# Windowed attention scores on four 32x32 parts of TensorE in place of two 64x64 parts, with the q tiles written by ScalarE and not placed by DMA

## The reference, cut to what matters

```python
q = Wq @ layernorm(x) + bq;  k = Wk @ ctx + bk;  v = Wv @ ctx + bv      # 128 x 1024
k, v padded by 8 left and 7 right                                       # WINDOW = 16
dots[h, t, w] = sum_d q[h, d, t] * k[h, d, t + w] / sqrt(16)            # 8 heads of 16 channels
out[h, d, t]  = sum_w softmax_w(dots)[h, t, w] * v[h, d, t + w]
x = x + Wo @ out + bo
z = layernorm(x);  gate = softmax(z @ gate_w.T), the best 2 of 8, renormed
x = x + sum_e w[:, e] * (z @ A[e].T @ B[e].T)                           # rank 64, 8 experts
```

## Time and profile before

| | before |
|---|---|
| device time, median of 3 runs | 1184.99 us (1182.85 to 1186.56) |
| device time of the profiled execution | 1181.87 us |
| its span, first to last instruction | 1180.1 us |
| TensorE matmuls busy, weight loads busy | 1118.5 us (95%), 965.0 us (82%) |
| VectorE, ScalarE, GpSimd busy | 904.6, 391.8, 408.9 us |
| matmul records on line 342 (scores) | 8192, busy 264.0 us |
| DMAs of `place_q` | 256 of 64 KB |

### The profile page before, as it was taken

The page is one execution under the profiler, slowest core; times in us unless marked ns, Lnnn a source line. Parts: engine busy times, 40 slices in busy tenths (PEclk is TensorE's granted clock), DMA queues, the critical chain, the costliest instruction groups (busy, mean ns, idle before and its releaser), DMA issues.

```text
span 1180.1 us, 38884 instructions
## 1 busy us (share of the span) xinstructions
PE 1118.5 (95%) x16384; PEld 965.0 (82%) x16384; DVE 904.6 (77%) x2021; ACT 391.8 (33%) x553; POOL 408.9 (35%) x302
## 2 busy tenths in 40 slices
PE   1677999999999999999999999999999999999987
PEld 1566888888888888888888888888888888888875
DVE  3576787877778787787878787888778787877763
ACT  3323433333333333333332333323333333233221
POOL 4443333333323334333333433333343233333210
PEclk9988999999999999999999999999999999999999
DMA  7344334455443355443345543434554433454200
GB/s 226 68 90 90 93 86 79 91 109 104 89 96 81 72 108 109 94 96 93 77 81 110 109 89 95 94 70 92 110 108 90 95 86 75 97 110 91 56 37 36
DMA packets 423345, 108.68 MB, mean 92 GB/s; under 512 B 405904, under 2 KB 406032, under 8 KB 423056
## 3 DMA queue, kind: packets, MB, share of 16 engines
q1 hardware_dynamic: 423184, 106.11, 41.6%
HBM read 55.22 MB, written 16.78 MB: 61 GB/s over the span
## 4 chain that ended last, share of the span: by engine, by line
PE 83%; DVE 4%; issue 4%; POOL 4%; SPq 3%; ACT 1%; DMA 1%; DVEq 0%; POOLq 0%; ACTq 0%
PE bank_a L314 29%; PE bank_b L342 19%; PE bank_c L314 15%; PE bank_b L363 14%; PE bank_a L372 4%; PE bank_b L332 2%; SPq L240 2%; DMA raw<-x 1%; DVE stats L616 1%; POOL prob L842 1%; SPq L249 1%; POOL attn_split L863 1%; POOL src_split L857 1%; POOL src_split L848 1%; ACT k_sb L591 1%
## 5 line engine op out<-in xcount | busy, mean ns | idle before, releaser
L342 PEld LDWEIGHTS bank_b<-k_sb,q_diag 64*64 64x64 f32 x8192 | 249.8, 135 | 29.6 <-issue 29.6
L342 PE MATMUL bank_b<-k_sb,q_diag 64*64 64x32 f32 x8192 | 264.0, 220 | 0.0
L842 POOL TENSOR_TENSOR prob<-prob,row_inv 128x512 f32<-128x512 f32 x128 | 134.2, 1048 | 262.1 <-DVE row_inv L705 262.1
L314 PE MATMUL bank_a<-down_split,mid_split 128*128 128x264 f32 (+1 forms) x1536 | 216.8, 291 | 1.8 <-DVE mid_split L748 1.8
L363 PEld LDWEIGHTS bank_b<-prob_t,v_diag 64*64 64x64 f32 x4608 | 187.6, 133 | 25.8 <-issue 16.4
L314 PE MATMUL bank_c<-src_split,w_split 128*128 128x512 f32 x576 | 161.9, 418 | 49.0 <-ACT k_sb L591 22.8
L363 PE MATMUL bank_b<-prob_t,v_diag 64*64 64x96 f32 (+2 forms) x4608 | 201.7, 238 | 0.9 <-DMA v_diag<-v_t 0.9
L314 PEld LDWEIGHTS bank_a<-down_split,mid_split 128*128 128x128 f32 x1536 | 191.4, 188 | 7.1 <-ACT mid_split L545 1.9
L314 PE MATMUL bank_a<-up_split,ht_split 128*128 128x512 f32 x768 | 188.7, 395 | 1.5 <-DVE ht_split L787 1.5
L528 ACT ACTIVATE prob<-prob 128x512 f32<-128x512 f32 x128 | 80.8, 631 | 296.5 <-DVE prob L693 294.7
L314 PEld LDWEIGHTS bank_c<-src_split,w_split 128*128 128x128 f32 x576 | 107.5, 196 | 81.0 <-ACT k_sb L591 32.4
(11 more groups left out here) (68 smaller groups left out, 1100.8 us busy)
## 6 DMA issues: line engine op xcount, KB each, us to landing
v_diag<-v_t SPq DMA_DIRECT2D x128, 132.0 KB, 5.4
raw<-x SPq DMA_DIRECT2D x32, 512.0 KB, 4.4
raw<-ctx SPq DMA_DIRECT2D x32, 512.0 KB, 5.8
q_diag<-q_xn SPq DMA_DIRECT2D x256, 64.0 KB, 3.6
resid_pair<-x SPq DMA_DIRECT2D x32, 512.0 KB, 3.2
out<-resid_pair SPq DMA_DIRECT2D x32, 512.0 KB, 2.6
v_diag<-up_w SPq DMA_DIRECT2D x1, 2048.0 KB, 10.6
prob_t<-down_w SPq DMA_DIRECT2D x1, 780.0 KB, 6.2
```

Of the source, the lines that this page charges most:

```text
L314: return nc.tensor.matmul(dst, st[:, s, st_cols], mv[:, m, mv_cols], start=start and n == 0, stop=stop and n == 2)
L342: last = nc.tensor.matmul(bank_b[m % 2][rows, t * KT:(t + 1) * KT], q_diag[rows, cur.parity, n, :], keys[rows, n * QT:n * QT + KT], start= ...
L842: nc.gpsimd.tensor_tensor(weights_of(m), weights_of(m), row_inv[:, cols].unsqueeze(2).broadcast_to([P, CT, KT]), ALU.mult).then_inc(prob_d ...
```

## The change

`scores_chunk` goes over four parts of 32 rows and 32 columns (`PAIRS`, `PW`), with two heads in each, where it went over two of 64. `q_diag` is half as wide: 32 columns for each tile, the even head's 16 queries and then the odd head's. ScalarE writes it straight from PSUM in two instructions, one for even and one for odd heads, over all 128 rows: scale and bias are per row, and are zero on the rows of the other heads, so that the zeros are written with them. `place_q`, its semaphore and the memset at the start go, the second layernorm has a buffer of its own, and the waits on the placing are waits on ScalarE's two writes.

```diff
-        q_diag = sb("q_diag", [P, 2, TILES, HALF_P])
+        q_diag = sb("q_diag", [P, 2, TILES, PW])
-        bq_scaled = sb("bq_scaled", [P, 1])
-        consts = sb("consts", [P, 4 + EXPERTS])
+        bq_scaled = sb("bq_scaled", [P, 2])
+        consts = sb("consts", [P, 6 + EXPERTS])
...
-            def place_q(ahead):
-
-                tiles = q_xn2[:].rearrange("p (n i) -> p n i", i=QT)
-                for h in range(HEADS):
-                    rows = slice(HD * h, HD * (h + 1))
-                    at = HD * h % HALF_P
-                    sp.dma_start(q_diag[rows, ahead.parity, :, at:at + QT],
-                                 tiles[rows]).then_inc(q_placed, 16)
...
-                if ahead:
-                    if ahead.c == 0:
-                        sp.wait_ge(q_diag_zero, 1)
-                    sp.wait_ge(q_out, ahead.count(1, 1))
-                    place_q(ahead)
...
-                    for z in range(HALVES):
-                        rows = slice(z * HALF_P, (z + 1) * HALF_P)
+                    for g in range(PAIRS):
+                        rows = slice(PW * g, PW * (g + 1))
                         last = nc.tensor.matmul(bank_b[m % 2][rows, t * KT:(t + 1) * KT],
                                                 q_diag[rows, cur.parity, n, :],
                                                 keys[rows, n * QT:n * QT + KT], start=False,
...
-                            pe.wait_ge(q_placed, cur.count(16 * HEADS, 16 * HEADS))
+                            pe.wait_ge(q_out, cur.count(2, 2))
...
-            nc.scalar.activation(bq_scaled[:], bias[:, 0:1], ACT.Copy, scale=SCALE).then_inc(bq_ready, 1)
+            for h in range(2):
+                nc.scalar.activation(bq_scaled[:, h:h + 1], bias[:, 0:1], ACT.Copy,
+                                     scale=consts[:, 4 + h:5 + h]).then_inc(bq_ready, 1)
...
-                    nc.scalar.activation(q_xn2[:], bank_c[:], ACT.Identity, bias=bq_scaled[:],
-                                         scale=SCALE).then_inc(q_out, 1)
+                    for h in range(2):
+                        nc.scalar.activation(q_diag[:, ahead.parity, :, h * QT:(h + 1) * QT],
+                                             bank_c[:].rearrange("p (n i) -> p n i", i=QT), ACT.Identity,
+                                             bias=bq_scaled[:, h:h + 1],
+                                             scale=consts[:, 4 + h:5 + h]).then_inc(q_out, 1)
...
-                    if ahead:
-                        act.wait_ge(q_placed, ahead.count(16 * HEADS, 16 * HEADS))
-                    nc.scalar.activation(q_xn2[:], resid[prev.parity], ACT.Identity, bias=shift[:, 1:2],
+                    nc.scalar.activation(xn2[:], resid[prev.parity], ACT.Identity, bias=shift[:, 1:2],
...
-            nc.gpsimd.memset(q_diag[:].rearrange("p a n c -> p (a n c)"), 0.0).then_inc(q_diag_zero, 1)
...
+    consts[:, 4:6] = consts[:, 0:2] * SCALE
```

More of the change, by code:

```diff
@@ L124, in build @@
         resid = [resid_pair[:, n * T:(n + 1) * T] for n in range(2)]
-        q_xn2 = sb("q_xn2", [P, T])
+        xn2 = sb("xn2", [P, T])
         k_sb = [sb("k_sb0", [P, KPAD]), sb("k_sb1", [P, KPAD])]
@@ L162, in build @@
         pads_zero = sem("pads_zero")
-        q_diag_zero, v_diag_zero = sem("q_diag_zero"), sem("v_diag_zero")
+        v_diag_zero = sem("v_diag_zero")
         prob_zero = sem("prob_zero")
@@ L167, in build @@
         stored = [sem("stored0"), sem("stored1")]
-        q_placed, v_placed = sem("q_placed"), sem("v_placed")
+        v_placed = sem("v_placed")
         q_done, k_done, v_done = sem("q_done"), sem("k_done"), sem("v_done")
@@ L413, in step @@
                         pe.wait_ge(result_done, old.count(2, 0))
-                    transposes(bank_a, q_xn2, range(0, 4)).then_inc(xt_done, 1)
+                    transposes(bank_a, xn2, range(0, 4)).then_inc(xt_done, 1)
                 if prev:
@@ L417, in step @@
                 if old:
-                    transposes(bank_a, q_xn2, range(4, FK)).then_inc(xt_done, 1)
+                    transposes(bank_a, xn2, range(4, FK)).then_inc(xt_done, 1)
                 if prev:
@@ L466, in step @@
                     if ahead:
-                        pe.wait_ge(q_out, ahead.count(1, 1))
+                        pe.wait_ge(q_out, ahead.count(2, 2))
                     elif cur:
@@ L554, in step @@
                     if ahead.c == 0:
-                        act.wait_ge(bq_ready, 1)
-                    nc.scalar.activation(q_xn2[:], bank_c[:], ACT.Identity, bias=bq_scaled[:],
-                                         scale=SCALE).then_inc(q_out, 1)
+                        act.wait_ge(bq_ready, 2)
+                    for h in range(2):
[3 more added lines that the diff above has]
+                                             scale=consts[:, 4 + h:5 + h]).then_inc(q_out, 1)
                     if ahead.c == 0:
@@ L661, in choose_experts @@
                 for n in range(2):
-                    nc.vector.tensor_scalar(pick[:, n, :], consts[:, 4:4 + EXPERTS],
+                    nc.vector.tensor_scalar(pick[:, n, :], consts[:, 6:6 + EXPERTS],
                                             top_atf[:, n:n + 1], gate[:, 3 + n:4 + n],
@@ L888, in shape_constants @@
     mask_cols = np.where(inside | (rows[:, None] >= QT), 0.0, MASKED).astype(np.float32)
-    consts = np.zeros((P, 4 + EXPERTS), np.float32)
+    consts = np.zeros((P, 6 + EXPERTS), np.float32)
     consts[:, 0] = rows // HD % 2 == 0
@@ L893, in shape_constants @@
     consts[:, 3] = EPS
-    consts[:, 4:] = np.arange(EXPERTS)
+    consts[:, 4:6] = consts[:, 0:2] * SCALE
+    consts[:, 6:] = np.arange(EXPERTS)
     return np.eye(P, dtype=np.float32), np.concatenate([mask_rows, mask_cols], axis=1), consts
```

## The result

The changed kernel takes 1239.12 us (median of 4 runs, 1232.48 to 1247.03) against 1185.78 us for the kernel before: ratio 1.0457, 95% interval 1.0384 to 1.053. It is 4.6% slower. The profiled execution is the slowest of its four: 1247.03 us, span 1245.1, 65.0 us more than the 1180.1 before.

What follows compares the result with a forecast made beforehand. TensorE was taken to bound the kernel, its steady part busy 1004.2 of 1005 us. Scores +20.8 us and the pipe's filling -6.2 us made +14.6 us on 1184.99: 1199 us predicted, 1.2% slower, range 1150 to 1350.

Steps and rivals of the forecast that it cites:

- the forecast's own mechanism: Whole kernel: dearer scores outweigh the gain while the pipe fills; 1199 us, own range 1190 to 1215, chance 0.45.
- rival 2: Score matmuls: each has a least cost whatever its width, deciding from about 16 ns upward; 1267 to 1419 us, chance 0.26.
- the scores' term: Score chunks on TensorE: 128 records at 15.9 ns against 64 at 29.25 ns, 0.163 us more a chunk, +20.8 us.
- four parts can't all be filled: Score matmuls: TensorE seems to take them in order, so the parts add no parallelism beyond what 29.25 ns already holds.
- the other premise: Score matmuls: 32-wide weights load in half the 64-wide time, 13.4 for 26.75 ns, plus a fixed 2.5 ns.
- Rival 3: Score matmuls: the four parts run side by side, a tile's 8 records take 64 ns, 109 us less; 1070 us, chance 0.16.
- TensorE's steady part should still be free of gaps: Sign in the profile after: no gaps on TensorE in the steady part, each step 0.65 us longer.
- The two writes: ScalarE's q writes: 2.50 us in place of 1.12, +1.4 us a step, hidden because the exponentials wait for VectorE.
- The filling of the pipe: Start of the kernel, before about 100 us: a shorter memset and VectorE's waits for x gone, -6.2 us (bounds 0.6 and 7.5).
- VectorE's three waits for x: First three steps: VectorE idles 3.76, 1.04 and 2.06 us for x; these waits should be gone in the profile after.
- Rival 4: q's 256 placing DMAs share queues with ctx and v tiles; worth nothing on TensorE's side unless rival 3 holds; no chance given.

Runs made afterwards that it cites:

- e9: The changed kernel with the two loops of a score chunk swapped, so that products in a row use the same 32x32 part: 1596.92 us, ratio 1.3497.
- e4: The changed kernel with 64 one-column matmuls (128 instructions) ahead of TensorE's first work: 1175.33 us, ratio 0.9943 to the kernel before.
- e8: The changed kernel with 96 one-column matmuls ahead of TensorE's first work: 1187.22 us, ratio 1.0018 to the kernel before.
- e10: The kernel of e6 with 48 one-column matmuls in front in place of 64: 1178.28 us, ratio 0.9961 to the kernel before.
- e3: The changed kernel with nearly all of the v placement left out, so its values are wrong: 1193.03 us.
- e5: The changed kernel with v_diag also written by ScalarE, in two instructions, and no placing DMA left: 1191.5 us, ratio 1.007 to the kernel before.
- e2: The kernel before, q still placed by DMAs, with only the scores on four 32x32 parts: 1278.09 us, ratio 1.0785.
- e1: The kernel before with q_diag written by ScalarE in four instructions, no placing DMA, scores still on two 64x64 parts: 1181.99 us, ratio 0.9979.
- e6: The kernel of e5 with 64 one-column matmuls ahead of TensorE's work: 1143.48 us, ratio 0.9677 to the kernel before.

## Why the prediction was right and where it was wrong

The sign was right and the range, 1150 to 1350, holds 1239. Both were luck. The mechanism behind the forecast is refuted: the sum came to a loss because one term was too dear by 102 us (+20.8 forecast, -81.4 measured), and one that cost more than that, the stops with 103.5 us and the clock with 44.4, was missing. The two errors nearly cancel. The measured time also lies outside the 1190 to 1215 that I gave the forecast's own mechanism, in the stretch that I had given to rival 2.

**The failed step: the scores' term, +20.8 us, through "four parts can't all be filled".** It measured -81.4 us. From the two matmuls that had begun by 606.90 I took it that TensorE's order keeps more than two parts from working together. That row can't show it: at the steady pace of 29.25 ns, two starts in 0.05 us are all that there can be. With four parts the starts are 9.04 ns apart, with one part 30.2 ns (e9), so the order doesn't bind. By the same run the other premise, that a 32-wide record costs half of a 64-wide one, isn't borne out either way: 32-wide records on one part take 30.2 ns each, 64-wide ones on two parts in turn 29.25, and 64-wide ones on one part, which would tell width from overlap, were not run. A tile's 8 records take 72 ns, and each part's own two fit into that at 36 ns each. Rival 3 had this right, 64 ns for the 72 measured, and 109 us of gain for 81 in the busy time, part of which is spent at the half clock. The Trainium skill ("TensorE: Matmul & The Clock Gate", Part 3) has four row parts, with 512 moving columns, at 3.07 times one; these traces have 3.3 times for four parts that differ in rows and columns, with 32 moving columns, so near it in another case. Its other rule that I weighed ("TensorEngine Tiling (Array Packing)", Instruction Overhead), 60 cycles for each matmul, doesn't hold for matmuls on different parts: 9.04 ns are 22 cycles. Rival 2, a least cost of 16 ns or more for a matmul, which the measured time seems to favour, is wrong too.

**What no part of the prediction held: TensorE's own code.** The instruction queue stood on the page of the kernel before, at 0.9% of the DMA engines, and I passed it over as a share. The need is not in the share but in the burst: 256 instructions in 1.2 us. Shown: the stops lie 256 instructions or a multiple of that apart in the program, and end 1.20 to 1.66 us after a code packet has landed; their places move with the program (e4, e8, e10); they shrink with less DMA traffic (e3, e5) and are longer where q is placed by DMA (e2); they go when the same instructions take longer (e9). That a piece is asked for when the one ahead of it begins is read from the packets' times alone, one packet behind each crossing in the kernel before; the asking itself isn't in a trace.

**The clock.** "TensorE's steady part should still be free of gaps" is the sentence that I gave as a test, and it failed. The loop of the changed kernel has 26 stops of over 1.5 us, one in each step; 22 of them have the clock at its lower level during the stop or within 2 us of its end, and 4 don't (the one that ends at 587.32 is followed by 1.00). After 101 us the lower level holds for 94 us, for 6 us in the kernel before. It costs 44.4 us on `down` and values alone.

**ScalarE.** The two writes take 2.30 us together for the 2.50 forecast. They are hidden: the exponentials behind them still wait for VectorE, 3.20 us. Right.

**The filling of the pipe, -6.2 us.** VectorE's three waits for x are gone. The first statistics start at 28.81 us for 31.76, 2.95 earlier, with 3.1 forecast. The half of the change that holds it, e1, gives 0 to 5 us by its interval, 2.5 by its ratio: right in mechanism, too large in size.

**Rival 4, the placing's traffic,** I put at nothing unless rival 3 came true. Rival 3 came true in pace, and then the placing did count, 39 us (e2): its idle time is under issue in front of scores, where late code shows, and not in waits for ctx.

## What to carry to other kernels

When a change makes short instructions shorter or doubles their number, look at how long 256 of the bound engine's instructions last where they are densest, and compare it with the time in which a piece of code arrives, here some 3 us with little traffic and 6.4 us (3.98 + 0.96 + 1.45) with much; an average share of the instruction queue says nothing. If an engine idles under "issue" in the middle of a run of equal instructions, move the program by some instructions and see whether the time moves: it costs one line. Look at where the stops go as well as at the time, and try more than one shift. For the same reason, two versions that differ in a few instructions of such an engine can differ by 3% or more through the places of the boundaries and the packets that these ask for (e6 and e10). And small DMA packets that nobody waits for aren't free once code is short.

## What was not expected of the hardware

- A steady step with runs of matmuls on one 32x32 part, TensorE busy 43.5 of 44 us, got a granted clock of 0.85 (e9), while four parts in turn (e6, 0.988 over the whole run) or two 64x64 ones (e1, 0.990) held it. The Trainium skill ("TensorE: Matmul & The Clock Gate", Part 1) ties the clock to how busy TensorE has been; here its records cover all but 0.5 us and the clock fell all the same. Why it fell was not tried further.
- A shift of the program by 16 matmuls, in one of some 24600, moved the time by 35 us (e6 to e10), and by 64 matmuls by 64 us (e4).
- A piece of code came up to 5 us late (the longest stops were 4.8 us, in e2 and in the changed kernel). With the v traffic gone (e3, e5) its packet still started a median of 1.8 to 2.9 us behind the crossing at the two places, for 0.63 in the kernel before. What holds it up there, where only x, ctx and results are on the DMA engines, is open.
